# A graph network with counted edges: GpSimd waits for each count unit, the unit leaves PSUM two slots behind its last chunk, and SyncE issues the edge loads

## The chip, the core and the metric

The kernel runs on one core of a Trainium2 chip. The metric is device time in microseconds (us); the median of several executions counts. Engine names: TensorE (PE in the profile, PEld its weight load), VectorE (DVE), ScalarE (ACT), GpSimd (POOL), SyncE (SP). A name with a q behind it is the engine's sequencer, which issues DMAs.

## What is computed

Four layers of a graph network over 6,250 nodes, 100,000 edges and 128 features. Layers 0 and 1 add a message with the edge's attributes for every edge; layers 2 and 3 add the plain row of the source node.

```python
h = relu(layernorm(x))
for l in range(2):                      # layers 0, 1
    msg = relu(h[src] + edge_attr)
    agg = segment_sum(msg, dst)
    h = batchnorm((h + agg) @ W1[l] + b1[l]) * gamma[l] + beta[l]
    h = relu(relu(relu(h) @ W2[l] + b2[l]))
x = x + h
h = relu(layernorm(x))                  # layers 2, 3, twice, with a relu between
    agg = segment_sum(h[src], dst)
    h = relu(((1 + eps) * h + agg) @ wA.T + bA) @ wB.T + bB
x = x + h
```

`src` and `dst` are the same in all layers, and `dst` is sorted. This is what the count matrices use.

## The kernel before

**Turns and slots.** The edges of layers 0 and 1 are worked off in 49 turns a layer, numbered 0 to 48 in layer 0 and 49 to 97 in layer 1. A turn has four slots, a slot is 512 edges, four for each of the 128 partitions. A slot is also numbered through: slot u of turn n is 4n + u.

**Gathers.** For each slot GpSimd issues four indirect DMAs (L675), each of which fetches 128 rows of the node table into `xg`, a ring of three turns. Its only wait in a layer is that the turn three before has been summed (L672). At the start of layer 1 it waits for the table of the layer before. Two slots of each layer (slot 2 of turns 26 and 48) are left out: their rows are loaded one by one by SyncE (L573), 24 rows a turn. So a layer has 776 gathers.

**Sums and messages.** ScalarE copies a slot's edge attributes to PSUM (L759), VectorE adds the gathered rows (L1131, which waits for the slot's gathers and raises `summed`), and ScalarE applies the relu to two slots at once (L786). After the fourth slot VectorE adds the windows of an earlier turn (L1030), then builds this turn's one-hot matrix of targets (L1077). With it TensorE scatters the messages: 32 matmuls a turn (L1510, `edge_windows`). When they are done, the buffer of the attributes is free, and ScalarE issues the load for three turns later (L751, L752, `load_behind`), 1.05 MB.

**Counts for layers 2 and 3.** During layers 0 and 1 matrices are built that say how often each source occurs near each target. A chunk is 128 edges; there are 544, 274 of them in layer 0. VectorE makes the one-hot of the source rows for a turn's chunks (L1096, `src_hot`, a ring of two turns) and, in slots 1 to 3, two or three chunks' cells (L1117, a ring of six chunks in `cell_room`). TensorE multiplies the two into the four banks of `psA` (L1494, `build_counts`): four matmuls for a piece, which is a chunk, or half of one where a unit ends in its middle. A unit is a run of chunks; there are 96, 26 in layer 0 of up to 16 chunks, 70 in layer 1, of three to six. When a unit is complete, ScalarE copies it from `psA` to `count_out` (L742), and SyncE stores it (L587). The next unit's first matmul waits for that copy. `cells_used` counts the pieces that TensorE has multiplied.

**The order.** Each engine has a queue written out by hand. TensorE does, in turn n, all chunks of the turn, then the turn's scatter. ScalarE copies a unit in the slot in which its last chunk's cells are made. VectorE does, in a turn: source rows, then for each slot cells and sum, then the windows. The preparation of all indices stands ahead of layer 0's turns on VectorE and TensorE, and GpSimd gathers meanwhile.

**Between and behind.** After a layer's edges two products with the weights and a batch norm follow for all nodes, and the rows are written to the table. Layers 2 and 3 multiply the count matrices with the features (L1537) and gather only the edges that the counts leave over (L695).

## Time and profile before

| | us |
|---|---|
| median of 3 runs | 2755.7 |
| lowest and highest | 2754.37, 2758.44 |
| the profiled execution, its own time | 2753.93 |
| its span in the profile | 2752.1 |
| layer 0, GpSimd's first to last gather | 13 to 988 |
| layer 1, the same | 1032 to 2001 |
| layers 2 and 3 and what stands around them | 2001 to 2752 |

The page gives each engine's busy time, the chain of work that ended last, and groups of like instructions; the trace answers with the instructions in order of time. An engine's idle time just before an instruction is shown with what ended it; "issue" means that nothing in the profile did. Idle time of an engine that isn't the last costs nothing. The granted clock of TensorE is a share of 2.4 GHz.

### The profile page before, as it was taken

To read this page: it belongs to the slowest core of one execution; us is meant where nothing else is said; L and a number is where in the kernel's file an instruction comes from. 1 tells how busy PE (TensorE), PEld (TensorE's weight loads), DVE (VectorE), ACT (ScalarE), POOL (GpSimd) and SP (SyncE) were. 2 spreads that over 40 slices of the span, in tenths; PEclk is the share of its full clock that TensorE was granted. 3 is DMA by queue.
4 is the path that set the end of the run, shared out by engine and by line. 5 is a ranking of instruction groups with operands and counts; after the bars stand their busy time and mean duration, and the time that the engine had idled before them with its cause. 6 is when DMAs were issued, how large, how long until landed. Compare 5 with 4: busy or idle time off the path is not lost.

```text
span 2752.1 us, 35065 instructions
## 1 busy us (share of the span) xinstructions
PE 1908.3 (69%) x9399; PEld 1278.4 (46%) x9399; DVE 1701.1 (62%) x2880; ACT 735.4 (27%) x1002; POOL 1941.4 (71%) x2048
## 2 busy tenths in 40 slices
PE   2476656566656672666566666656578999989999
PEld 2354444344444442435444444434444566546555
DVE  7797677777777764777777777777774221342212
ACT  4132222222222251333333333333361000210001
POOL 6777777777777727777777777777707777377773
PEclk8687777787888786878878888888878999999999
DMA  6343433343434333444444444444426566465653
GB/s 199 97 144 107 129 107 122 113 128 114 135 114 136 120 112 98 132 138 127 149 128 149 135 156 141 156 149 149 146 92 203 190 219 198 135 208 186 211 193 101
DMA packets 228544, 396.82 MB, mean 144 GB/s; under 512 B 43080, under 2 KB 133020, under 8 KB 228388
## 3 DMA queue, kind: packets, MB, share of 16 engines
q0 software_dynamic: 65024, 133.30, 18.1%
q1 hardware_dynamic: 111684, 162.15, 17.2%
q10 hardware_dynamic: 51680, 99.63, 10.4%
q8 instruction: 57, 0.93, 0.1%
q14 instruction: 99, 0.81, 0.1%
HBM read 333.10 MB, written 61.81 MB: 143 GB/s over the span
## 4 chain that ended last, share of the span: by engine, by line
POOL 52%; PE 22%; issue 18%; DVE 4%; DMA 3%; ACT 1%; DVEq 1%; POOLq 0%; SPq 0%; ACTq 0%
POOL xg L675 50%; PE psA L1537 14%; PE psG L1552 4%; POOL xg L695 2%; DMA xg<-node_table,src_all 2%; PE psG L1601 2%; PE psA L1609 1%; DVE xp_room L1131 0%; DVE hid L1077 0%; PE psG L1631 0%; DVE acc L1030 0%; DVE hid L1247 0%; PE psA L1618 0%; DVE xp_room L955 0%; DVEq L1052 0%
## 5 line engine op out<-in xcount | busy, mean ns | idle before, releaser
L675 POOL DMA_INDIRECT xg<-node_table,src_all x1520 | 1437.3, 946 | 506.9 <-issue 458.3
L1510 PE MATMUL psG<-hid,xp_room 128*128 128x160 f32 x3072 | 614.2, 376 | 421.6 <-DVE hid L1077 411.7
L1510 PEld LDWEIGHTS psG<-hid,xp_room 128*128 128x128 f32 x3072 | 595.3, 255 | 466.3 <-issue 455.8
L1494 PE MATMUL psA<-cell_room,xp_room 128*128 128x512 f16 (+1 forms) x2336 | 551.6, 388 | 299.2 <-ACT count_out L742 253.3
L1117 DVE TENSOR_SCALAR cell_room<-psG,cell_all 128x932 f16<-128x932 int16 x1088 | 684.6, 688 | 0.0
L695 POOL DMA_INDIRECT xg<-node_table,idx x480 | 468.1, 975 | 250.6 <-issue 248.7
L759 ACT COPY psG<-xp_room 128x512 f32<-128x512 f32 x384 | 226.5, 590 | 1257.7 <-DVE xp_room L1131 1226.5
L1494 PEld LDWEIGHTS psA<-cell_room,xp_room 128*128 128x128 f16 x2336 | 230.7, 103 | 582.7 <-ACT count_out L742 287.8
L1131 DVE TENSOR_TENSOR xp_room<-psG,xg 128x512 f32<-128x512 f32 x380 | 257.3, 677 | 385.8 <-DMA xg<-node_table,src_all 372.2
L1030 DVE TENSOR_TENSOR acc<-acc,row_slot 128x38 f32 x192 | 38.7, 202 | 385.3 <-ACT row_slot L838 360.7
L1077 DVE SCALAR_TENSOR_TENSOR hid<-loc_all,round_off,psG 128x2560 f32<-128x2560 f32 x96 | 274.7, 2862 | 0.1
L1537 PE MATMUL psA<-cell_room,xp_room 128*128 128x456 f16 x1200 | 241.7, 361 | 21.8 <-DVE xp_room L1253 21.8
L1537 PE MATMUL psA<-hid,xp_room 128*128 128x456 f16 x1152 | 234.8, 364 | 0.0
L786 ACT ACTIVATE xp_room<-xp_room 128x1024 f32<-128x1024 f32 x196 | 206.0, 1052 | 7.6 <-DVE xp_room L1023 4.5
L1030 DVE TENSOR_TENSOR acc<-acc,psG 128x160 f32 x272 | 87.3, 321 | 193.2 <-issue 148.3
L1537 PEld LDWEIGHTS psA<-cell_room,xp_room 128*128 128x128 bf16 x1200 | 115.7, 97 | 142.8 <-issue 26.6
L742 ACT CAST count_out<-psA 128x1862 f16<-128x1862 f32 x96 | 163.3, 1701 | 57.1 <-PE psA L1494 57.0
L1537 PEld LDWEIGHTS psA<-hid,xp_room 128*128 128x128 bf16 x1152 | 111.8, 97 | 118.4
L1552 PE MATMUL psG<-rows_h,xg 128*128 128x160 f32 x960 | 136.3, 299 | 6.2 <-DMA xg<-node_table,idx 6.2
L1552 PEld LDWEIGHTS psG<-rows_h,xg 128*128 128x128 f32 x960 | 133.6, 190 | 10.3 <-DMA xg<-node_table,idx 7.2
L838 ACT COPY row_slot<-psA 128x456 f32<-128x456 f32 x16 | 8.6, 538 | 360.2 <-PE psA L1537 360.2
L1096 DVE TENSOR_TENSOR xp_room<-psG,src_lo_all 128x768 f16<-128x768 int16 (+2 forms) x132 | 93.2, 727 | 0.0
(156 smaller groups left out, 804.5 us busy)
## 6 DMA issues: line engine op xcount, KB each, us to landing
xp_room<-in_edge_attr_dram ACTq DMA_DIRECT2D x95, 768.0 KB
cell_room<-count_store SPq DMA_DIRECT2D x16, 2850.0 KB
count_store<-count_out SPq DMA_DIRECT2D x96, 465.5 KB
hid<-count_store SPq DMA_DIRECT2D x16, 2736.0 KB
xg<-node_table,src_all POOLq DMA_INDIRECT x1520
xp_room<-in_edge_attr_dram ACTq DMA_DIRECT2D x95, 256.0 KB
row_slot<-node_table SPq DMA_DIRECT2D x1024, 0.5 KB
hid<-node_table SPq DMA_DIRECT2D x1024, 0.5 KB
```

The source lines that it names most:

```text
L675: nc.gpsimd.indirect_dma_start(xg[:, n % XG, u, j, :], None, x if n < RAW_TURNS else table, bass.IndirectOffsetOnAxis(ap=src_all[:, s, j:j ...
L695: nc.gpsimd.indirect_dma_start(xg[:, q, u, j, :], None, table, bass.IndirectOffsetOnAxis(ap=idx[:, q, u, j:j + 1], axis=0),).then_inc(row_ ...
L742: act.copy(count_out[:, k % 2, :], psA[:, :, :].rearrange("p k c -> p (k c)")[:, 0:CB]).then_inc(count_evicted, 1)
L759: act.copy(ea_stage, ea[:, n % RING, u, :, :].rearrange("p j d -> p (j d)")).then_inc(ea_staged, 1)
L786: act.activation(half, half, ACT.Relu).then_inc(msg_ready, 1)
L1077: nc.vector.scalar_tensor_tensor(out=rows.rearrange("p u j w -> p (u j) w"), in0=loc.unsqueeze(2).broadcast_to((P, SLOTS * EPP, WIN)), sca ...
L1117: nc.vector.tensor_scalar(cells[:, c % CELL_RING, c0:c1], iota_bank[:, 0:c1 - c0], float(c0), cell_all[:, c:c + 1], ALU.add, ALU.is_equal) ...
L1131: nc.vector.tensor_tensor(ea[:, n % RING, u, :, :].rearrange("p j d -> p (j d)"), ea_stage, rows, ALU.add).then_inc(summed, 1)
L1494: last = nc.tensor.matmul(psA[:, bank, 0:w], src_hot[:, hots(n) % 2, at, :], cells[:, c % CELL_RING, c0:c0 + w], start=first, stop=end)
L1510: last = nc.tensor.matmul(psG[:, q, h * WIN:(h + 1) * WIN], ea[:, t, u, j, :], rows[:, u, j, :], start=(u == slots[0] and j == 0), stop=(u ...
L1537: last = nc.tensor.matmul(out_cols, xp[:, b, part, :], counts[h][:, :, i * CW:(i + 1) * CW], start=(b == 0 and part == 0), stop=(b == BLOC ...
L1552: last = nc.tensor.matmul(psG[:, q, h * WIN:(h + 1) * WIN], xg[:, q, u, j, :], late_hot[:, q, u * EPP + j, :], start=(u == slots[0] and j ...
```

## The change

It concerns layers 0 and 1.

- **GpSimd waits.** Each unit has a gate: the slot two behind the one in which its last chunk's cells are made, and at least two behind the gate before (`UNIT_GATE`). Before the gathers of the slot behind a gate GpSimd waits until TensorE has multiplied the unit. Where two gates stand more than six slots apart, further gates are put between them, for the chunks whose step lies two slots back (`BURST_GATE`). There are 109 gates, 39 in layer 0 and 70 in layer 1.
- **Units** are copied out by ScalarE at their gate, no longer in the slot of their last chunk.
- **TensorE** takes chunks slot by slot (`STEPS`). A piece of the next unit is moved behind the gate of the unit before. A turn's scatter stands behind the first slot of the turn that follows. Turns 0 and 1 keep their order.
- **Rings:** twelve chunks of cells (six of them in `rows_h`, for which VectorE waits until the table is written), source rows of three turns.
- **Chunks** are spread over one turn fewer; the last two turns of a layer have none.
- **SyncE** issues the attributes' loads (`load_ahead`), at a turn's start, ahead of its rows and stores.

```diff
-CELL_RING = 6
+CELL_RING = 12
+ROOM_CELLS = 6
+HOT_RING = 3
+LAG_SLOTS = 2
+LONGEST_BURST = 6
...
-COUNT_TURNS = TURNS - 1 - RAW_TURNS
+COUNT_TURNS = TURNS - 2 - RAW_TURNS
...
+def unit_gates():
+
+    gates, last = [], -1
+    for k in range(UNITS):
+        built = SLOT_OF[(UNIT_END[k] - 1) // 2]
+        stop = (built // SLOTS // TURNS + 1) * TURNS * SLOTS - SLOTS - 1
+        last = min(max(built + LAG_SLOTS, last + 2), stop)
+        gates.append(last)
+    return gates
...
+def piece_step(c, p0):
+
+    k = UNIT_OF[2 * c + p0 // HALF]
+    return max(SLOT_OF[c], UNIT_GATE[k - 1] + 1) if k > 0 else SLOT_OF[c]
...
+def burst_gates():
+
+    gates = {g: UNIT_USED[k] for k, g in enumerate(UNIT_GATE)}
+    for layer in range(2):
+        bounds = [(layer * TURNS + RAW_TURNS) * SLOTS - 1] + [g for g in UNIT_GATE if g // SLOTS // TURNS == layer]
+        for a, b in zip(bounds, bounds[1:]):
+            parts = -(-(b - a) // LONGEST_BURST)
+            for i in range(1, parts):
+                g = a + (b - a) * i // parts
+                gates[g] = max(USED_AFTER[c] for c in range(CHUNKS) if piece_step(c, PIECES[c][-1][0]) <= g - LAG_SLOTS)
+    return gates
...
 # SyncE
+            def load_ahead(n):
+
+                if not RING <= n < EDGE_TURNS:
+                    return
+                used = n - RING
+                sp.wait_ge(scattered[used % 2], sp.snap(rounds * (used // 2 + 1) + 1))
+                load_turn(n)
...
                 for n in range(layer * TURNS, (layer + 1) * TURNS):
-                    for k in units_in(turn_chunks(n)):
-                        sp.wait_ge(count_evicted, k + 1)
-                        sp.dma_start(count_store[k], count_out[:, k % 2, :]).then_inc(count_stored[k % 2], 16)
+                    load_ahead(n + 1)
                     gather_rows(layer, n % TURNS)
+                    for u in range(SLOTS):
+                        for k in units_at(n * SLOTS + u):
+                            sp.wait_ge(count_evicted, k + 1)
+                            sp.dma_start(count_store[k], count_out[:, k % 2, :]).then_inc(count_stored[k % 2], 16)
...
 # GpSimd
                     for u in range(SLOTS):
+                        if n * SLOTS + u - 1 in BURST_GATE:
+                            pool.wait_ge(cells_used, BURST_GATE[n * SLOTS + u - 1])
...
 # ScalarE
-                            if u == (SLOTS - 1 if n == RAW_TURNS else 1):
-                                load_behind(n - 1)
-                            units_out(slot_chunks(n, u))
+                            units_out(i)
...
 # VectorE
-                slot = hots(n) % 2
-                if n >= 2 and turn_chunks(n - 2):
-                    dve.wait_ge(cells_used, USED_AFTER[turn_chunks(n - 2)[-1]])
...
+                slot = hots(n) % HOT_RING
+                if n % TURNS == RAW_TURNS:
+                    dve.wait_ge(table_written, 16 * LG * (n // TURNS + 1))
+                if hots(n) > HOT_RING:
+                    dve.wait_ge(cells_used, USED_AFTER[turn_chunks(COUNTING[hots(n) - 1 - HOT_RING])[-1]])
...
 # TensorE
-                    build_counts(n)
-                    edge_windows(layer, n)
+                    for u in range(SLOTS):
+                        build_counts(n * SLOTS + u)
+                        if u == 0 and n > max(layer * TURNS, RAW_TURNS):
+                            edge_windows(layer, n - 1)
+                    if n < RAW_TURNS:
+                        edge_windows(layer, n)
+                edge_windows(layer, (layer + 1) * TURNS - 1)
```

## Rows read from the trace of the kernel before

**Rows 1.** The page: busy time by engine, then groups (busy, mean ns, idle before).

```profile
PE 1908.3 (69%) x9399; PEld 1278.4 (46%) x9399; DVE 1701.1 (62%) x2880; ACT 735.4 (27%) x1002; POOL 1941.4 (71%) x2048
...
L1494 PE MATMUL psA<-cell_room,xp_room 128*128 128x512 f16 (+1 forms) x2336 | 551.6, 388 | 299.2 <-ACT count_out L742 253.3
L1117 DVE TENSOR_SCALAR cell_room<-psG,cell_all 128x932 f16<-128x932 int16 x1088 | 684.6, 688 | 0.0
```

**Rows 2.** The page: the chain that ended last, by engine and by line.

```profile
POOL 52%; PE 22%; issue 18%; DVE 4%; DMA 3%; ACT 1%; DVEq 1%; POOLq 0%; SPq 0%; ACTq 0%
POOL xg L675 50%; PE psA L1537 14%; PE psG L1552 4%; POOL xg L695 2%; DMA xg<-node_table,src_all 2%; PE psG L1601 2%; PE psA L1609 1%; DVE xp_room L1131 0%; DVE hid L1077 0%; PE psG L1631 0%; DVE acc L1030 0%; DVE hid L1247 0%; PE psA L1618 0%; DVE xp_room L955 0%; DVEq L1052 0%
```

**Rows 3.** Groups of layer 1, 1032 to 2002 us: the gathers.

```profile
L675 POOL DMA_INDIRECT xg<-node_table,src_all x776 | 732.2, 944 | 280.0 <-issue 233.8 <-DMA node_table<-rows_h 43.8 <-DVE xp_room L1131 2.4
```

**Rows 4.** Timeline of GpSimd, layer 1's first gathers: start, us, what [idle before].

```profile
1031.87 0.94 POOL L675 DMA_INDIRECT xg<-node_table,src_all  x1 [43.76 <-DMA node_table<-rows_h]
1033.12 0.94 POOL L675 DMA_INDIRECT xg<-node_table,src_all  x1 [0.30 <-issue]
```

**Rows 5.** Timeline of GpSimd, the 48th and 49th gather of layer 0.

```profile
78.13 0.94 POOL L675 DMA_INDIRECT xg<-node_table,src_all  x1 [0.30 <-issue]
79.38 0.95 POOL L675 DMA_INDIRECT xg<-node_table,src_all  x1 [0.30 <-issue]
```

**Rows 6.** Timeline, 99 to 123 us: the sums of slots 8 and 12, the first chunks.

```profile
99.92 0.69 DVE L1131 TENSOR_TENSOR xp_room<-psG,xg 128x512 f32<-128x512 f32 x1 [8.00 <-ACT psG L759]
...
117.78 4.12 PE L1494 MATMUL psA<-cell_room,xp_room 128*128 128x512 f16 x20
...
122.28 0.67 DVE L1131 TENSOR_TENSOR xp_room<-psG,xg 128x512 f32<-128x512 f32 x1
```

**Rows 7.** Timeline, 1784 to 1808 us: the last slot of turn 86 and turn 87.

```profile
1784.68 0.94 POOL L675 DMA_INDIRECT xg<-node_table,src_all  x1 [0.30 <-issue]
...
1788.99 0.69 DVE L1131 TENSOR_TENSOR xp_room<-psG,xg 128x512 f32<-128x512 f32 x1 [3.57 <-DMA xg<-node_table,src_all]
...
1791.20 1.69 ACT L742 CAST count_out<-psA 128x1862 f16<-128x1862 f32 x1
...
1792.94 1.74 PE L1494 MATMUL psA<-cell_room,xp_room 128*128 128x512 f16 x4 [5.87 <-ACT count_out L742]
...
1795.03 6.19 PE L1510 MATMUL psG<-hid,xp_room 128*128 128x160 f32 x32 [0.35 <-DVE hid L1077]
...
1804.61 2.56 PE L1494 MATMUL psA<-cell_room,xp_room 128*128 128x512 f16 x12 [1.80 <-ACT count_out L742]
```

**Rows 8.** Windows over two of those units: busy by engine, PEclk, DMA share, GB/s.

```profile
1792.94:1794.68 1.74, 1.74 (x4) 0.44 (x4) 1.74 (x2) 0.00 (x0) 1.13 (x3) 0.50 0.48 155
1804.61:1807.17 2.56, 2.55 (x12) 1.08 (x12) 0.74 (x2) 0.43 (x1) 1.91 (x3) 1.00 1.05 394
```

**Rows 9.** Timeline, other turns: their last gather, their scatter; a unit of four pieces.

```profile
1390.16 0.94 POOL L675 DMA_INDIRECT xg<-node_table,src_all  x1 [0.30 <-issue]
...
1398.84 4.63 PE L1510 MATMUL psG<-hid,xp_room 128*128 128x160 f32 x32 [0.24 <-issue]
...
1704.97 3.35 PE L1494 MATMUL psA<-cell_room,xp_room 128*128 128x512 f16 x16 [1.80 <-ACT count_out L742]
...
1904.52 0.94 POOL L675 DMA_INDIRECT xg<-node_table,src_all  x1 [0.30 <-issue]
...
1915.31 7.47 PE L1510 MATMUL psG<-hid,xp_room 128*128 128x160 f32 x32 [6.02 <-DVE hid L1077]
```

**Rows 10.** Timeline: a turn's row loads on SyncE; the page: all DMA traffic.

```profile
1795.51 9.03 SPq L573 DMA_DIRECT2D hid<-node_table  x24
...
DMA packets 228544, 396.82 MB, mean 144 GB/s; under 512 B 43080, under 2 KB 133020, under 8 KB 228388
```

**Rows 11.** Timeline of GpSimd in layer 2: a gather behind waits.

```profile
2110.95 0.94 POOL L695 DMA_INDIRECT xg<-node_table,idx  x1 [0.87 <-issue]
```

More of the change, by code:

```diff
@@ L123, in slot_chunks @@
     return [c for i, c in enumerate(chunks) if 1 + i * (SLOTS - 1) // len(chunks) == u]
-def units_in(chunks):
-    return [UNIT_OF[e] for c in chunks for e in (2 * c, 2 * c + 1) if e + 1 in UNIT_END]
 def row_work(t):
@@ L173, in parted, with units_at @@
     return [c for c in chunks if len(PIECES[c]) > 1]
+COUNTING = [n for n in range(EDGE_TURNS) if turn_chunks(n)]
+TURN_OF = {c: n for n in COUNTING for c in turn_chunks(n)}
+SLOT_OF = {c: n * SLOTS + u for n in COUNTING for u in range(SLOTS) for c in slot_chunks(n, u)}
 def hots(n):
-    return sum(len(turn_chunks(t)) > 0 for t in range(n + 1))
+    return COUNTING.index(n) + 1
+def unit_gates():
[6 more added lines that the diff above has]
+    return gates
+UNIT_GATE = unit_gates()
+def piece_step(c, p0):
+    k = UNIT_OF[2 * c + p0 // HALF]
+    return max(SLOT_OF[c], UNIT_GATE[k - 1] + 1) if k > 0 else SLOT_OF[c]
+STEPS = {}
+for c in range(CHUNKS):
+    for p0, p1 in PIECES[c]:
+        STEPS.setdefault(piece_step(c, p0), []).append((c, p0, p1))
+def burst_gates():
[8 more added lines that the diff above has]
+    return gates
+BURST_GATE = burst_gates()
+def units_at(i):
+    return [k for k, g in enumerate(UNIT_GATE) if g == i]
 MOST_CHUNKS = max(len(turn_chunks(n)) for n in range(EDGE_TURNS))
@@ L188 @@
 LAYERS = 4
-assert TURNS % 2 == 1 and 2 * SLOTS * EPP * WIN <= CELL_RING * CB
+assert TURNS % 2 == 1 and 2 * SLOTS * EPP * WIN <= ROOM_CELLS * CB
 assert SUPERS % SLOTS == 0 and OVERLAP % EPP == 0 and SECOND <= P
@@ L193 @@
 assert CB % 2 == 0 and CB - IOTA <= IOTA <= 1024 and MOST_CHUNKS <= CELL_RING and EPP * D == 512
-assert CBANKS == 4 and UPG * CW <= 512 and HALF_B * UPG >= CELL_RING * BLOCKS // 2
+assert CBANKS == 4 and UPG * CW <= 512 and HALF_B * UPG >= ROOM_CELLS * BLOCKS // 2
 def group_blocks(g):
@@ L734, in centre_raw, with units_out @@
                     last.then_inc(raw_centred, 1)
-            def units_out(chunks):
-                for k in units_in(chunks):
+            def units_out(i):
+                for k in units_at(i):
                     act.wait_ge(cells_used, UNIT_USED[k])
@@ L1116, in chunk_cells @@
                 for c0, c1 in CELL_PARTS:
[L1117 removed]
+                    nc.vector.tensor_scalar(cells[c % CELL_RING][:, c0:c1], iota_bank[:, 0:c1 - c0],
                                             float(c0), cell_all[:, c:c + 1], ALU.add, ALU.is_equal
@@ L1475, in turn_rows, with build_counts @@
                     last.then_inc(cols_turned, 1)
-            def build_counts(n):
-                chunks = turn_chunks(n)
-                for i, c in enumerate(chunks):
-                    if i == 0:
-                        pe.wait_ge(src_hot_ready, hots(n))
-                    for p0, p1 in PIECES[c]:
-                        k = UNIT_OF[2 * c + p0 // HALF]
-                        first = 2 * c + p0 // HALF == UNIT_END[k] - UNIT_SIZES[k]
-                        end = 2 * c + p1 // HALF == UNIT_END[k]
-                        if first and k > 0:
-                            pe.wait_ge(count_evicted, k)
-                        pe.wait_ge(cells_ready, 2 * (c + 1))
-                        at = len(chunks) + parted(chunks).index(c) if p0 else i
-                        for bank in range(CBANKS):
-                            c0 = bank * 512
-                            w = min(512, CB - c0)
-                            last = nc.tensor.matmul(psA[:, bank, 0:w], src_hot[:, hots(n) % 2, at, :],
-                                                    cells[:, c % CELL_RING, c0:c0 + w], start=first, stop=end)
-                        last.then_inc(cells_used, 1)
+            def build_counts(i):
+                for c, p0, p1 in STEPS.get(i, ()):
+                    n = TURN_OF[c]
+                    chunks = turn_chunks(n)
+                    if c == chunks[0] and p0 == 0:
+                        pe.wait_ge(src_hot_ready, hots(n))
+                    k = UNIT_OF[2 * c + p0 // HALF]
+                    first = 2 * c + p0 // HALF == UNIT_END[k] - UNIT_SIZES[k]
+                    end = 2 * c + p1 // HALF == UNIT_END[k]
+                    if first and k > 0:
+                        pe.wait_ge(count_evicted, k)
+                    pe.wait_ge(cells_ready, 2 * (c + 1))
+                    at = len(chunks) + parted(chunks).index(c) if p0 else c - chunks[0]
+                    for bank in range(CBANKS):
+                        c0 = bank * 512
+                        w = min(512, CB - c0)
+                        last = nc.tensor.matmul(psA[:, bank, 0:w], src_hot[:, hots(n) % HOT_RING, at, :],
+                                                cells[c % CELL_RING][:, c0:c0 + w], start=first, stop=end)
+                    last.then_inc(cells_used, 1)
             def edge_windows(layer, n):
```

24 lines of the change are left out of this document (9 added, 15 removed).

## The prediction

> **What bounds the kernel now.** I read the page's chain first, because one engine is named in half of it: GpSimd, at the gather line of layers 0 and 1, L675, with 50% of the span; TensorE follows with 22%, nearly all of it in layers 2 and 3 [rows 2]. The busy shares do not say this: in the whole span GpSimd has 71%, TensorE 69%, VectorE 62% [rows 1]. Then I looked at the groups of layer 1 alone: 776 gathers, 732.2 us busy and 233.8 us of "issue" before them, so (732.2 + 233.8 + 2.4) / 776 = 1.248 us for each, and nothing else stands before a gather but one pause of 43.8 us [rows 3]. GpSimd thus never waits inside layer 0 or 1. A layer's time is 776 x 1.248 = 968 us plus the stretch between the last gather of one layer and the first of the next (43.76 us after layer 0 [rows 4]). Everything else in these layers is hidden: VectorE builds cells with no idle before them at all [rows 1], and TensorE's 253.3 us of waiting for ScalarE's evictions [rows 1] is idle time of an engine that is not last.
>
> So a wait put into GpSimd's queue is free only if it is already met when GpSimd comes to it. If it is not, all later gathers of the layer move, and so does the layer's end. That is the question for each of the 109 gates.
>
> **First gate.** The diff's formulas, filled in with the constants, give layer 0 39 gates (26 of units, 13 between) and layer 1 70, all of units. The first stands after slot 3 of turn 2 (slot 11): before slot 12's gathers GpSimd waits for two chunks used. Now GpSimd starts slot 12's first gather at 79.38 us: it is the 49th, after 48 of twelve slots [rows 5]. VectorE and TensorE are far behind at that point, because the preparation of indices comes first in their queues: VectorE sums slot 8 at 99.92 us and slot 12 at 122.28 us, and TensorE multiplies its first chunks from 117.78 us on, twenty matmuls in 4.12 us, so that the second chunk (eight matmuls) is used at 117.78 + 8/20 x 4.12 = 119.4 us [rows 6]. Nothing in the change brings it forward: turn 1's scatter still stands before it on TensorE, since turns 0 and 1 keep their order. GpSimd then waits 119.4 - 79.4 = **40 us**. Before the change it used this time to run up to three turns ahead, as deep as the buffers of xg allow, and VectorE caught up behind it. That lead is what the gate takes away; the gathers are the bound from then on, so nothing gives it back. Queued behind the wait are all later gathers, and VectorE waits for them.
>
> **Later gates, layer by layer.** A unit's matmuls can't begin before the unit before it is evicted, and that now happens at that unit's gate slot. Between two gates TensorE must therefore do: landing of the gate slot's gathers, VectorE's sum, ScalarE's eviction, all matmuls of the next unit, and, where a turn ends between, the scatter of 32 matmuls. GpSimd takes 8 gathers, 9.98 us, for a distance of two slots. Forty gates have this distance. I priced them with turn 86 and what follows it, taking 1785.62 us (1784.68 + 0.94, the last gather of turn 86) as zero [rows 7].
>
> Twelve gates stand after slot 2 and their predecessor after slot 0. Their unit stands behind the scatter on TensorE, which ends at 1795.03 + 6.19 = 1801.22, that is at 15.6. A late unit has three or four pieces of four matmuls; three take 2.56 us [rows 7], four take 3.35 [rows 9], mean 2.95. It is used at 18.55; GpSimd is there after three slots, 12 x 1.248 = 14.98. Loss 3.55 each, 12 x 3.55 = **43 us**. VectorE's next turn then hangs on gathers that are as much later, so the loss returns each turn.
>
> Fourteen gates (one of them layer 0's last) stand after slot 1, with the predecessor after slot 3 of the turn before. Here the unit goes ahead of the scatter, but must wait for the eviction, which ends at 1791.20 + 1.69 = 1792.89, at 7.27. After this wait TensorE is slow: a piece that follows 5.87 us of idle takes 1.74 us [rows 7], at a granted clock of 0.50 (1.2 GHz), where the next unit's three pieces, close behind a scatter, had 1.00 (2.4 GHz) and took 0.85 each [rows 8]. With pieces some 1.6 us apart, 3.5 of them end at 7.27 + 5.6 = 12.87; GpSimd is there at 9.98. Loss 2.9 each, 14 x 2.9 = **41 us**.
>
> The other fourteen of distance two come after slot 0 or 3; their eviction isn't behind a scatter, and the stall before has already given them 3 us, so I cost them at nothing, as I do all gates of three slots or more: these have 5 us more than the cases above, whose losses are under 4. If that cover were gone, each us would cost 1 us at up to 14 gates.
>
> **Bounds of these two terms.** They depend on when the gathers land and on TensorE's clock. In a turn where landing was quick and TensorE warm the scatter ended at 1398.84 + 4.63 - 1391.10 = 12.4, and a gate after slot 2 would just be met; a warm unit after slot 3 ends at 7.27 + 2.95 = 10.2, 0.2 late. So the lower end is 0. In a slow turn the scatter ended at 1915.31 + 7.47 - 1905.46 = 17.3 [rows 9]: with 3.35 behind it 5.7 late, 12 x 5.7 = 68; four slow pieces of 1.74 end at 14.2, 4.25 late, 14 x 4.25 = 60. Upper end 128. I take 84, as turn 86 is near the middle of its neighbours.
>
> The Trainium skill (TensorE: Matmul & The Clock Gate, Part 1) says that "the default state is throttled, and activity releases the throttle". It speaks against this change, which breaks TensorE's work into units with a wait before each; the piece of 1.74 us at the clock 0.50 [rows 8] agrees with it.
>
> **What costs nothing.** *Loads by SyncE:* two issues a turn leave ScalarE's queue, which isn't last. On SyncE they stand behind the count stores of the turn before and ahead of 24 row loads (9.03 us of issue [rows 10]); with them a turn fills about half of 16 x 1.248 = 20 us. The latest load is issued after an eviction behind slot 3, at about 7.3; 1.05 MB at the mean 144 GB/s [rows 10] is 7.3 us, so it lands at 15.5, and its first reader on ScalarE comes one turn after zero, at 24. If this cover were gone, ScalarE's copies would hold up the sums. *Scatters a slot later:* they wait for the marks of VectorE now, and still do. *Rings of 12 cells and 3 row marks:* VectorE has no wait to lose there [rows 1]. *One turn fewer with chunks:* VectorE builds the same number. *Ends of layers and layers 2, 3:* the last gate is six slots or more before the end, so the 43.76 us stay as they are.
>
> **Sum.** 2753.9 (profiled execution, span 2752.1) + 40 + 43 + 41 = 2878; the median of the runs is 1.8 above the profiled one: **2879 us**.
>
> **Rivals.** (a) *Only the first gate costs*: landing quick and TensorE warm in nearly all turns, the lower ends. 2755.7 + 40 = 2796. For it: turns like the one at 1391. Against: a stalled GpSimd leaves TensorE more idle. 12%. (b) *TensorE slow throughout*: scatters of 7.47 and pieces of 1.6 in layer 1. Gates after slot 2 then lose 3.55 + 1.28 + 2.65 = 7.5, 12 x 7.5 = 90; 2755.7 + 40 + 90 + 41 = 2927. This is what the clock page of the Trainium skill leads to if the waits between units always lower the clock. 7%. (c) *A met wait costs GpSimd time too*: one gather of layer 2, whose turn starts with waits, came after 0.87 instead of 0.30 [rows 11]; 109 x 0.57 = 62, 2941. Against: the waits for `summed` that stand in layers 0 and 1 already, two a turn, cost nothing in [rows 3]. 4%. (d) *Not slower: a pause quickens the gathers behind it.* If descriptors pile up in a queue and the 0.30 before each gather is that queue, a pause drains it, and the four gathers behind each gate come without it: 109 x 4 x 0.30 = 131 us back, 2879 - 131 = 2748. It decides from 0.28 us per gather on (124 / 436). Against: after a pause of 43.76 us the next gather comes 1.25 us later, as always [rows 4]. 4%. (e) *The gates are met*, so nothing changes: 2756. It needs the second chunk 40 us earlier. 3%. The forecast has 70%.
>
> **Range and chances.** From (a) to the forecast with its upper bounds: 2755.7 + 40 + 128 = 2924; so 2796 to 2924. About 0.2% is what a measurement of this kernel can tell from no change. Slower 0.93, within 0.2% 0.03, faster 0.04.
>
> **What would show it.** In the changed kernel's trace: one wait of about 40 us on GpSimd, near 79 us, released by TensorE's count matmuls; in layer 0 hardly another; in layer 1 some 25 waits of 2 to 6 us on the same line, by the end of it mostly once a turn; VectorE's idle before its sums up by the same sum; layers 2 and 3 and the ends of layers as long as now; gathers still 1.25 us apart. I am wrong if GpSimd's waits sum to under 30 us, if gathers change their pace, or if the time is lost at waits of ScalarE for loads.

## The result and the profile after

| | before | after |
|---|---|---|
| median, us | 2755.0 | 2895.0 |
| lowest and highest | 2752.2, 2758.4 | 2889.5, 2898.1 |
| span of the profiled execution | 2752.1 | 2891.7 |
| layer 0, GpSimd's first to last gather | 13 to 988 | 13 to 1021 |
| layer 1, the same | 1032 to 2000 | 1066 to 2141 |

The changed kernel takes 1.0509 times as long [1.0497, 1.0521]: 140 us more. Layer 0 is 33 us longer, layer 1 106 us; the stretch between the layers and everything behind layer 1 are as long as before, within 1.2 us. (Layer 1's last gather of before ends at 2000.4, not 2001.)

The page of after, its chain by engine and by line, then the groups of the gathers and of VectorE's sums (busy, mean ns, idle before and what ended it):

```profile
POOL 37%; PE 32%; issue 15%; DMA 8%; DVE 6%; DVEq 2%; ACT 1%; POOLq 0%; SPq 0%; ACTq 0%
POOL xg L743 35%; PE psA L1598 15%; DMA xg<-node_table,src_all 7%; PE psG L1566 6%; PE psG L1613 4%; PE psA L1550 4%; DVE hid L1133 2%; PE psG L1662 1%; POOL xg L763 1%; DVEq L1108 1%; PE psA L1670 1%; DVE acc L1086 1%; DVE xp_room L1187 0%; PE psG L1692 0%; ACT count_out L810 0%
...
L743 POOL DMA_INDIRECT xg<-node_table,src_all x1520 | 1439.1, 947 | 647.9 <-issue 449.9
...
L1187 DVE TENSOR_TENSOR xp_room<-psG,xg 128x512 f32<-128x512 f32 x380 | 257.3, 677 | 524.1 <-DMA xg<-node_table,src_all 518.8
```

The same sums in the page of before:

```profile
L1131 DVE TENSOR_TENSOR xp_room<-psG,xg 128x512 f32<-128x512 f32 x380 | 257.3, 677 | 385.8 <-DMA xg<-node_table,src_all 372.2
```

VectorE stands idle 138 us longer before its sums, which is GpSimd's lost time passed on. The gathers are L743 now. One takes 947 ns (946 before), but GpSimd holds only 37% of the chain, where it had 52% [rows 2]; TensorE has 32%, DMA 8% (3% before), VectorE 6%. So in a part of layer 1 the end is set by a chain that runs through several engines. Where GpSimd stood, its waits tell (total us, times, longest); first the stretch of layer 0 behind the preparation, then layer 1:

```profile
POOL xg L743 <- issue: 222.5, 730, 0.3
POOL xg L743 <- PE psA L1550: 35.9, 5, 32.2
```

```profile
POOL xg L743 <- issue: 226.2, 742, 0.3
POOL xg L743 <- PE psA L1550: 114.7, 30, 7.0
```

"issue" is the 0.30 us ahead of each gather that [rows 3] showed. Behind TensorE's count matmuls (L1550) GpSimd now waits 35.9 us in layer 0, 32.2 of them at one gate, and 114.7 us at 30 gates of layer 1. Less the usual 0.30 each, that is 34.4 + 105.7 = 140 us, the whole difference. In what follows "layer 1's waits" is this sum, less 0.30 for each.

**The first gate.** The timeline at the gate that stands behind slot 11 (start, us, what, [idle before]):

```profile
84.52 0.59 ACT L818 COPY psG<-xp_room 128x512 f32<-128x512 f32 x1 [8.95 <-DVE first_i L1100]
...
90.56 0.67 DVE L1187 TENSOR_TENSOR xp_room<-psG,xg 128x512 f32<-128x512 f32 x1
...
108.00 4.92 PE L1550 MATMUL psA<-cell_room,xp_room 128*128 128x512 f16 x24
...
110.02 0.94 POOL L743 DMA_INDIRECT xg<-node_table,src_all  x1 [32.23 <-PE psA L1550]
111.27 0.94 POOL L743 DMA_INDIRECT xg<-node_table,src_all  x1 [0.30 <-issue]
```

VectorE sums slot 8 at 90.56 us, where it stood at 99.92 before, and the second chunk is used at about 110, where 119.4 was worked out from [rows 6]. The wait is 32.2 us.

**One turn of layer 1.** From one gate behind slot 2 to the next, a turn later:

```profile
1867.74 1.71 ACT L810 CAST count_out<-psA 128x1862 f16<-128x1862 f32 x1 [1.53 <-PE psA L1550]
1867.97 0.94 POOL L743 DMA_INDIRECT xg<-node_table,src_all  x1 [6.75 <-PE psA L1550]
...
1869.47 0.37 SPq L654 DMA_DIRECT2D count_store<-count_out  x1
...
1869.89 0.43 SPq L615 DMA_DIRECT2D xp_room<-in_edge_attr_dram  x1
1870.36 0.71 SPq L616 DMA_DIRECT2D xp_room<-in_edge_attr_dram  x1
...
1871.71 0.94 POOL L743 DMA_INDIRECT xg<-node_table,src_all  x1 [0.30 <-issue]
...
1877.94 0.69 DVE L1187 TENSOR_TENSOR xp_room<-psG,xg 128x512 f32<-128x512 f32 x1 [9.92 <-DMA xg<-node_table,src_all]
...
1879.99 0.78 DVE L1086 TENSOR_TENSOR acc<-acc,psG 128x160 f32 x2 [1.35 <-issue]
...
1880.82 2.86 DVE L1133 SCALAR_TENSOR_TENSOR hid<-loc_all,round_off,psG 128x2560 f32<-128x2560 f32 x1
...
1883.98 6.11 PE L1566 MATMUL psG<-hid,xp_room 128*128 128x160 f32 x32 [11.91 <-DVE hid L1133]
...
1889.93 2.55 PE L1550 MATMUL psA<-rows_h,xp_room 128*128 128x512 f16 x12
...
1893.13 0.95 POOL L743 DMA_INDIRECT xg<-node_table,src_all  x1 [5.49 <-PE psA L1550]
```

This is the chain, and it closes on itself. The gate opens at 1867.97. Slot 3's four gathers end at 1871.71 + 0.94 = 1872.65. They land at 1877.94, 5.3 us later, when VectorE can add them. Windows and one-hot matrix take until 1883.98, the scatter and the three pieces of the next unit until 1889.93 + 2.55 = 1892.48, and GpSimd goes on at 1893.13: 25.16 us for a turn whose 16 gathers need 16 x 1.248 = 19.97. Waits of 6.75 and 5.49 us at gates one turn apart show that the loss doesn't die away; each late slot 3 makes the next unit late. Note the two loads of SyncE (L615, L616), issued while slot 3 is being gathered: they stand behind the store of the unit (L654), which waits for ScalarE's copy of it (L810), which TensorE's last piece releases together with the gate. Windows of the gathers' own time and of the landing (us, busy by engine with counts, PEclk, DMA share, GB/s):

```profile
1867.97:1872.65 4.68, 2.53 (x12) 1.10 (x12) 0.05 (x1) 1.48 (x1) 3.77 (x4) 1.00 0.53 140
1872.65:1877.94 5.29, 0.00 (x0) 0.00 (x0) 0.00 (x0) 0.00 (x0) 3.77 (x5) 0.90 0.80 253
```

In the 5.29 us of landing no engine but GpSimd works; the DMA engines are 0.80 busy with 253 GB/s.

### The profile page after: what moved, and what is told of

Same layout as the page of the kernel before. It is cut to its first block, busy times and chain, and to the rows that moved or that the text cites. A ratio compares the mean times of both kernels' runs of the same rounds, so it can differ in the third digit from the quotient of the medians.

```text
span 2891.7 us, 35118 instructions
## 1 busy us (share of the span) xinstructions
PE 1882.2 (65%) x9399; PEld 1265.4 (44%) x9399; DVE 1700.1 (59%) x2878; ACT 733.3 (25%) x1002; POOL 1939.4 (67%) x2048
## 4 chain that ended last, share of the span: by engine, by line
POOL 37%; PE 32%; issue 15%; DMA 8%; DVE 6%; DVEq 2%; ACT 1%; POOLq 0%; SPq 0%; ACTq 0%
POOL xg L743 35%; PE psA L1598 15%; DMA xg<-node_table,src_all 7%; PE psG L1566 6%; PE psG L1613 4%; PE psA L1550 4%; DVE hid L1133 2%; PE psG L1662 1%; POOL xg L763 1%; DVEq L1108 1%; PE psA L1670 1%; DVE acc L1086 1%; DVE xp_room L1187 0%; PE psG L1692 0%; ACT count_out L810 0%
## 5 line engine op out<-in xcount | busy, mean ns | idle before, releaser
L743 POOL DMA_INDIRECT xg<-node_table,src_all x1520 | 1439.1, 947 | 647.9 <-issue 449.9
L1566 PE MATMUL psG<-hid,xp_room 128*128 128x160 f32 x3072 | 588.2, 365 | 639.4 <-DVE hid L1133 610.3
L1566 PEld LDWEIGHTS psG<-hid,xp_room 128*128 128x128 f32 x3072 | 570.5, 245 | 669.6 <-issue 636.8
L1550 PE MATMUL psA<-rows_h,xp_room 128*128 128x512 f16 (+1 forms) x1156 | 284.3, 401 | 144.5 <-ACT count_out L810 126.0
L1550 PE MATMUL psA<-cell_room,xp_room 128*128 128x512 f16 (+1 forms) x1180 | 276.3, 385 | 112.8 <-ACT count_out L810 96.9
L1173 DVE TENSOR_SCALAR cell_room<-psG,cell_all 128x932 f16<-128x932 int16 (+1 forms) x548 | 345.1, 686 | 0.0
L1173 DVE TENSOR_SCALAR rows_h<-psG,cell_all 128x932 f16<-128x932 int16 (+1 forms) x540 | 340.3, 686 | 0.0
L1550 PEld LDWEIGHTS psA<-rows_h,xp_room 128*128 128x128 f16 x1156 | 120.4, 107 | 293.0 <-ACT count_out L810 134.4
L1550 PEld LDWEIGHTS psA<-cell_room,xp_room 128*128 128x128 f16 x1180 | 118.7, 103 | 250.4 <-ACT count_out L810 104.5
L810 ACT CAST count_out<-psA 128x1862 f16<-128x1862 f32 x96 | 163.0, 1698 | 13.5 <-PE psA L1550 13.5
```

What stands on the lines that cost most here:

```text
L743: nc.gpsimd.indirect_dma_start(xg[:, n % XG, u, j, :], None, x if n < RAW_TURNS else table, bass.IndirectOffsetOnAxis(ap=src_all[:, s, j:j ...
L810: act.copy(count_out[:, k % 2, :], psA[:, :, :].rearrange("p k c -> p (k c)")[:, 0:CB]).then_inc(count_evicted, 1)
L1173: nc.vector.tensor_scalar(cells[c % CELL_RING][:, c0:c1], iota_bank[:, 0:c1 - c0], float(c0), cell_all[:, c:c + 1], ALU.add, ALU.is_equal) ...
L1550: last = nc.tensor.matmul(psA[:, bank, 0:w], src_hot[:, hots(n) % HOT_RING, at, :], cells[c % CELL_RING][:, c0:c0 + w], start=first, stop=end)
L1566: last = nc.tensor.matmul(psG[:, q, h * WIN:(h + 1) * WIN], ea[:, t, u, j, :], rows[:, u, j, :], start=(u == slots[0] and j == 0), stop=(u ...
```

## The experiments

The ratio is to the kernel before, timed beside each. Layer 1's waits as above, from the one profiled execution of each kernel; the first gate took 29 to 34 us in all kernels that keep the change's gates and SyncE's loads.

| kernel | median, us | ratio, interval | layer 1's waits |
|---|---|---|---|
| after | 2895.0 | 1.0509 [1.0497, 1.0521] | 105.7 |
| e1_no_gates | 2755.2 | 1.0005 [0.9995, 1.0014] | none |
| e2_first_gate | 2795.6 | 1.0147 [1.0130, 1.0163] | none |
| e4_gates_late | 2776.9 | 1.0082 [1.0065, 1.0099] | none |
| e3_loads_scalar | 2868.4 | 1.0417 [1.0396, 1.0437] | 65.7 |
| e5_sync_early | 2875.4 | 1.0429 [1.0411, 1.0446] | 81.1 |
| e8_small_loads | 2843.4 | 1.0326 [1.0309, 1.0343] | 54.4 |
| e11_short_scatters | 2879.2 | 1.0453 [1.0436, 1.0471] | 76.5 |
| e12_both_small | 2839.3 | 1.0304 [1.0287, 1.0322] | 47.3 |
| e9_warm_scatters | 2953.2 | 1.0725 [1.0707, 1.0743] | 154.2 |
| e10_warm_units | 2910.9 | 1.0565 [1.0547, 1.0583] | 117.5 |
| e6_three_rows | 2748.3 | 0.9968 [0.9957, 0.9980] | none |
| e7_four_rows | 2848.0 | 1.0325 [1.0308, 1.0343] | other waits |

### Do GpSimd's waits cost it all?

**The change without them:**

```diff
 # after
-                        if n * SLOTS + u - 1 in BURST_GATE:
-                            pool.wait_ge(cells_used, BURST_GATE[n * SLOTS + u - 1])
```

> The changed kernel without GpSimd's 109 waits; all the rest of the change stays (evictions at the gate slots, scatters a slot later, loads by SyncE, the larger rings). Theory A (the whole loss is GpSimd standing at its gates): 2755 us, within 4 us of the kernel before, and no wait before a gather but the one between the layers. Theory B (the new order of TensorE and the late evictions cost time by themselves): over 2775 us, with VectorE or TensorE in the chain of the edge layers in place of the gathers.

It took 2755.15 us, 1.4 more than before, and the interval of the ratio includes 1. So later evictions, scatters a slot later, the longer rings and SyncE's loads cost nothing that can be told from noise (0.14% at most, 4 us) as long as GpSimd does not wait. That holds only for a GpSimd that runs ahead; the loads come back below.

**The first wait alone,** in the kernel before:

```diff
 # before
+                        if n * SLOTS + u == 12:
+                            pool.wait_ge(cells_used, 2)
```

> The kernel before with one wait added: before the gathers of slot 12 GpSimd waits for two pieces used. Theory A (lead that is lost at the start is never given back, the gathers being the bound): the wait ends when the second chunk is used, 119.4 us in the kernel before, so 40 us of wait and 2755 + 40 = 2795 us. Rival (the layer has slack behind its start, VectorE being far behind anyway): much of it is given back, 2760 to 2775 us.

GpSimd's wait in its trace:

```profile
POOL xg L677 <- PE psA L1496: 41.6, 1, 41.6
```

41.6 us of waiting, and 2795.57 - 2753.77 = 41.8 us of time: a wait at 79 us is paid in full, and nothing in the 2,700 us behind it gives it back. This kernel keeps ScalarE's loads, and its wait is the 40 us of the prediction; the change's is 32.2.

**All waits two slots later:**

```diff
 # after
-                        if n * SLOTS + u - 1 in BURST_GATE:
-                            pool.wait_ge(cells_used, BURST_GATE[n * SLOTS + u - 1])
+                        if n * SLOTS + u - 3 in BURST_GATE:
+                            pool.wait_ge(cells_used, BURST_GATE[n * SLOTS + u - 3])
```

> The changed kernel with each of GpSimd's waits two slots later (four slots behind the last chunk); evictions and TensorE's order as in the changed kernel. Theory A: a wait that is met costs nothing, and two slots (9.98 us) are more than any loss of a later gate (6.5 us), so only the first gate costs, and there GpSimd comes 10 us later to a count that is reached at 109.7 us: 21 us of wait, 2755 + 21 = 2776 us. Theory B (waits or order cost by themselves): over 2800 us.

2776.9. The first gate waits 22.5 us; before no other is GpSimd idle for more than its usual 0.30. So a wait that is met costs GpSimd nothing, at over a hundred gates, and the loss of layer 1 is a matter of less than two slots (10 us) at each gate.

### Why layer 1 lost more than it should: the loads

The gathers of slot 3 landed later than in [rows 7]. Theory C puts this on SyncE's loads, theory D on TensorE's clock. Landing is counted from the end of a slot's last gather to the sum's start, mean of slot 3 in turns 85 to 96: 3.39 us before, 4.93 after.

**Loads by ScalarE again,** at their old place:

```diff
 # after, SyncE
-                    load_ahead(n + 1)
...
 # ScalarE
+                            if u == (SLOTS - 1 if n == RAW_TURNS else 1):
+                                load_behind(n - 1)
                             units_out(i)
```

> The changed kernel with the attributes' loads back on ScalarE, at their old place behind the scatter; the gates stay. Theory C (the twelve gates after slot 2 lose 5.5 us each in place of 3.55 because SyncE's load now starts with the released gathers and slot 3's gathers land late): landing of slot 3 in the last turns back from 4.9 to 3.4 us behind the last gather, some 1.5 to 2 us less at each of 12 gates and about 10 us less at the others, but the first gate back to 40 us from 32, since VectorE's first sums stand behind ScalarE's wait for the first scatter again: 2895 - 18 - 10 + 8 = 2875 us. Theory D (TensorE's clock is what makes the gates late): only the first gate changes, 2903 us.

2868.4: 26.6 us less than the change. Landing falls to 2.27 us, layer 1's waits from 105.7 to 65.7, while the first gate rises to 41.9, as in the kernel with the first wait alone (41.6). So the new issuer of the loads costs layer 1 40 us and gives 9 back at the start.

**Loads by SyncE, but earlier,** ahead of the count stores of the turn:

```diff
 # after, SyncE
-                    load_ahead(n + 1)
                     gather_rows(layer, n % TURNS)
                     for u in range(SLOTS):
+                        if u == 1:
+                            load_ahead(n + 2)
```

> The changed kernel with SyncE's load moved ahead of the turn's count stores: it is issued in turn n for turn n + 2, as soon as turn n - 1 is scattered, on the same queue of SyncE. Theory C1 (the time of issue is what counts: behind the last eviction the load runs beside the gathers that have just been released): landing of slot 3 and the waits of layer 1 as with the loads on ScalarE (66 us in place of 106), the first gate as in the changed kernel (32 us): 2895 - 40 = 2855 us. Theory C2 (the queue is what counts: loads, rows and stores behind one another on SyncE): no change, 2895 us.

2875.4, between the two. Landing is shorter than in the change and with ScalarE's loads, 1.90 us, so it is the load's moment that held up slot 3, not the engine that issues it. But only 25 of the 40 us come back: gates behind slot 1 lose 39.6 us here and lost 9.9 in the change. Slot 3's gain was partly another slot's loss.

The moment can be read in six of the traces. Here is turn 87 of the kernel before, slot 3's first gather and ScalarE's load:

```profile
1800.90 0.94 POOL L675 DMA_INDIRECT xg<-node_table,src_all  x1 [0.30 <-issue]
1801.26 0.39 ACTq L751 DMA_DIRECT2D xp_room<-in_edge_attr_dram  x1
```

Means of turns 85 to 94, us; the load's issue is counted from the start of slot 3's first gather (its last one ends 4.7 behind that start):

| kernel | load issued | landing of slot 3 |
|---|---|---|
| e3_loads_scalar | 2.4 ahead | 2.38 |
| e5_sync_early | 2.4 ahead | 1.94 |
| before | 1.2 behind | 3.63 |
| after | 2.1 behind | 5.15 |
| e4_gates_late | 5.0 behind | 1.91 |
| e1_no_gates | 5.3 behind | 2.37 |

Where the load goes out ahead of the four gathers or behind their end, they land in about 2 us; where it goes out among them, in 3.6 and 5.2. The kernel before had such loads too; the change put them 0.9 us later. These kernels differ in their waits as well, so the table alone does not show the cause. That called for taking the load's traffic away altogether.

**Loads an eighth as large,** at the change's own place:

```diff
 # after, SyncE
+                parts = 16 if n >= TURNS + RING else P
-                sp.dma_start(ea[:, t, 0:SLOTS - 1, :, :].rearrange("p u j d -> p u (j d)"), slots).then_inc(ea_loaded[t], 16)
+                sp.dma_start(ea[0:parts, t, 0:SLOTS - 1, :, :].rearrange("p u j d -> p u (j d)"), slots[0:parts]).then_inc(ea_loaded[t], 16)
```

and the same for the fourth slot.

> The changed kernel, except that in layer 1, from its fourth turn on, a load of attributes fetches 16 of the 128 partitions, so an eighth of its bytes and packets (the other partitions keep what the turn three before left there: seven eighths of the attributes are left out). Issue, waits and order stay. Theory C (what layer 1 loses is mostly the landing of slot 3's gathers, which the load's packets hold up): landing falls to 1.9 us or below, as with the early load, and now for the whole turn; at least the 40 us between the change (2895) and the kernel with ScalarE's loads come back, and as the other slots' landing is freed too, some 15 more: 2840, with layer 1's waits at 50 us. Rival (the load's bytes don't matter, only its place in a queue): 2895.

2843.4, 51.6 us less than the change, and layer 1's waits are 51.3 us shorter. The same stretches as above, in this kernel (slot 3's gathers after a gate, then their landing):

```profile
1842.46:1847.15 4.69, 2.53 (x12) 1.10 (x12) 1.95 (x4) 1.78 (x2) 3.77 (x4) 1.00 0.48 156
1847.15:1849.71 2.56, 0.00 (x0) 0.00 (x0) 0.00 (x0) 0.00 (x0) 1.88 (x2) 1.00 0.40 80
```

Landing takes 2.56 us where it took 5.29, at a DMA share of 0.40 instead of 0.80; both are turn 86. GpSimd's waits in layer 1:

```profile
POOL xg L744 <- PE psA L1551: 61.9, 25, 4.1
```

The issue, the waits and the order are the change's own; only the packets of the loads are gone. So these packets hold up the gathers that GpSimd has just been let go to issue: half of layer 1's loss. The Trainium skill (DMA: Bandwidth & Descriptors, Queues, rings and completion order) says that each DMA engine takes turns between the queues it has work for, a packet at a time. That would make a gather's packets share with a load's, and the landing of 5.29 and 2.56 us agrees. No run here shows whether the two share the engines or another part of the way.

### What of it is TensorE's clock?

**TensorE kept busy ahead of the scatter.** The bank may be written once VectorE has added its windows, so that wait comes first:

```diff
 # after, TensorE
+                    pe.wait_ge(window_added, pe.snap((rounds * n + r) * WINDOWS + (layer * 2 * WINDOWS + WINDOWS + 1)))
+                    for _ in range(32 if layer == 1 and n > TURNS + 2 else 0):
+                        nc.tensor.matmul(psG[:, q, 384:512], ident[:, :], ident[:, :], start=True, stop=True,
+                                         skip_group_check=True)
                     pe.wait_ge(hot_set[q], pe.snap(rounds * (n // 2) + r + (spare_sets(layer, q) + 1)))
-                    pe.wait_ge(window_added, pe.snap((rounds * n + r) * WINDOWS + (layer * 2 * WINDOWS + WINDOWS + 1)))
```

> The changed kernel; in layer 1, from its fourth turn on, TensorE multiplies the identity with itself 32 times (into columns of the window's bank that nothing uses) before each scatter, while it waits for VectorE's one-hot matrix. Extra work of 3.6 us at the full clock, beside an idle time of 316 us in 31 turns. Theory D (the low clock of the scatter carries part of the twelve gates behind slot 2): scatters go from 5.94 us (30 of 48 above 6) to 4.6, the twelve gates lose 1.4 us less each: 2895 - 17 = 2878. Rival: the extra work ends after the one-hot matrix in the turns with little idle time, and what is late there is given back: 2895 to 2915.

2953.2, far slower than either theory said. One turn of it:

```profile
1922.03 2.86 DVE L1133 SCALAR_TENSOR_TENSOR hid<-loc_all,round_off,psG 128x2560 f32<-128x2560 f32 x1
...
1922.04 10.13 PE L1561 MATMUL psG<-ident 128*128 128x128 f32 x64 [9.28 <-DVE acc L1086]
...
1932.00 4.51 PE L1569 MATMUL psG<-hid,xp_room 128*128 128x160 f32 x32
```

The scatter is at its full speed, 4.51 us at a granted clock of 1.00 (2.4 GHz), but 32 products of f32 are 64 matmuls in the trace and take 10.13 us, and they can't begin before the windows are added at 1922.03. The one-hot matrix is there at 1924.89; the scatter begins 7.1 us behind it. The loss was put on the chain, not taken off it.

**TensorE kept busy ahead of units** that start in slot 0:

```diff
 # after, TensorE
                     if first and k > 0:
+                        if i >= (TURNS + 3) * SLOTS and i % SLOTS == 0:
+                            done = i // SLOTS - 1
+                            pe.wait_ge(window_added, pe.snap(rounds * done * WINDOWS + (2 * WINDOWS + WINDOWS + 1)))
+                            for _ in range(16):
+                                nc.tensor.matmul(psG[:, done % 2, 384:512], ident[:, :], ident[:, :], start=True, stop=True,
+                                                 skip_group_check=True)
                         pe.wait_ge(count_evicted, k)
```

> The changed kernel; in layer 1, from its fourth turn on, TensorE multiplies the identity with itself 16 times (into columns of the window's bank that nothing uses) before the first piece of each unit that starts in slot 0, while it waits for ScalarE's copy of the unit before; ahead of that it waits until VectorE has added the windows of three turns before. 1.8 us at the full clock, 3.6 at half, beside an idle time of 5 to 7 us. Theory D (the low clock of pieces and scatter carries the loss behind such a copy): the pieces behind it take 0.85 us instead of 1.4 to 1.7 and the scatter behind them 4.5 instead of 6 to 7.5, so gates after slots 1 and 2 lose 2 to 3 us less: 2895 - 26 x 2 = 2843. Rival C (landing and the order of the work set it, the clock little): 2885 to 2895; if the multiplications themselves keep the clock low or end after the copy, 2895 to 2910.

2910.9. The extra products are busy for 90.3 us in layer 1, with twice as many matmuls as were meant, and gates behind slot 1 lose 45.4 us instead of 9.9. Neither run says what the clock costs, because each made TensorE late by more than a warm clock could give.

**Shorter scatters** instead, with no work added: 24 of 32 matmuls.

```diff
 # after, TensorE
+                parts = EPP - 1 if n >= TURNS + RING else EPP
...
-                            for j in range(EPP):
+                            for j in range(parts):
...
```

> The changed kernel, except that in layer 1, from its fourth turn on, a scatter takes three of a partition's four edges in each slot: 24 matmuls instead of 32 (a quarter of the messages is left out of the sums). In turns 85 to 96 a scatter of the change took 6.64 us, at the full clock it takes 4.5; 24 matmuls at the low clock would take 4.98. So this run gives TensorE nearly what a warm clock would, without extra work. Theory D (the low clock of the scatter carries part of the loss behind slot 2): twelve gates lose 1.7 us less each, 2895 - 20 = 2875. Rival (the gates wait for landing and sums, the scatter hides): 2893 to 2897.

2879.2: 15.8 us less, most of the 20 expected. The runs lie from 2871.3 to 2884.1, and the profiled one is the fastest. In it the twelve gates behind slot 2 lose 51.8 us instead of 66.1, 1.2 less each, and layer 1's waits are 29.2 us shorter in all: behind slot 3 they fall from 25.8 to 6.3, behind slot 1 they rise from 9.9 to 18.5. So the scatter's length lies on the chain, and with it what the low clock adds to it.

**Both cuts:**

> Both cuts: in layer 1, from its fourth turn on, loads of 16 of 128 partitions and scatters of 24 of 32 matmuls (seven eighths of the attributes and a quarter of the messages are left out). If landing and scatter are two terms of one path, their savings add: 2843 with small loads alone, less the 20 us of the short scatters: 2823, with layer 1's waits at about 33 us. If they hide behind each other, 2838 to 2843.

2839.3: only 4.1 us below the small loads alone, with intervals that touch. The savings do not add. The traces say why, at the twelve gates behind slot 2. From the end of a turn's last gather to GpSimd's start behind that gate there are four legs: the landing, the time from the sum to the scatter (windows and one-hot matrix), the scatter, and the rest (the unit, and until GpSimd starts). With the gate met GpSimd would start after 12 x 1.248 + 0.30 = 15.28 us. Means of the twelve, us:

| kernel | landing | to the scatter | scatter (granted clock) | the rest | sum less 15.28 | loss at the gate |
|---|---|---|---|---|---|---|
| after | 5.28 | 6.01 | 6.66 (0.69) | 2.85 | 5.52 | 5.51 |
| e11_short_scatters | 5.44 | 6.01 | 5.29 (0.66) | 2.85 | 4.31 | 4.31 |
| e8_small_loads | 2.59 | 6.00 | 6.68 (0.68) | 2.85 | 2.84 | 2.83 |
| e12_both_small | 2.54 | 6.01 | 6.03 (0.57) | 2.85 | 2.15 | 2.14 |

So landing and scatter are two legs of one path, and nothing hides. But with both cuts the shorter scatter ran at a lower mean clock, so it saved 0.65 us where it had saved 1.37. Layer 1's waits are 7.1 us shorter than with small loads alone; against that the first gate waited 33.5 us in this kernel's profile and 31.0 there.

### A way that does gain

GpSimd's pace sets layers 0 and 1 [rows 3], so fewer gathers should be time. Before had two slots a layer loaded as rows by SyncE. **Three:**

```diff
 # before
-ROW_TURNS = (26, TURNS - 1)
+ROW_TURNS = (19, 34, TURNS - 1)
-BY_SYNC = 6
+BY_SYNC = 9
```

> The kernel before, with three slots of each layer loaded row by row by SyncE in place of two (36 rows a turn in place of 24), so that GpSimd has 4 gathers fewer in each layer. Theory A (the number of gathers is all that sets the time of layers 0 and 1): 2 x 4 x 1.248 = 10 us less, 2744 us. Rival (VectorE's or SyncE's queue is right behind the gathers): 2750 us or more.

2748.3 us, 0.9968 of before [0.9957, 0.9980], so a small gain that is clear of noise: 8 gathers less, 8.7 us of the 10 expected. **Four** (`ROW_TURNS = (15, 26, 37, TURNS - 1)`, `BY_SYNC = 12`):

> The kernel before with four such slots (48 rows a turn; at 9.03 us per 24 rows and some 2.7 us of reading addresses ahead of them SyncE needs about 23 us a turn of 20). Theory A with SyncE's time: GpSimd would save 20 us, but rows that come late hold up the sums of their slots: 2740 to 2800 us; if SyncE's issue were no limit, 2734 us.

2848.0, 91 us slower than before. GpSimd's long waits in its trace:

```profile
POOL xg L695 <- issue: 301.3, 471, 118.5
POOL xg L675 <- DMA node_table<-rows_h: 80.1, 1, 80.1
POOL xg L675 <- DVE xp_room L1131: 28.7, 18, 9.9
```

The stretch between the layers has grown from 43.8 [rows 4] to 80.1, 28.7 us are spent waiting for sums (23.3 of them beyond the usual 0.30), and one gap in layer 2 of 118.5 us was 65.9 before. Together, 36.3 + 23.3 + 52.6 less 20 us for 16 gathers, they make 92 us where 91 were lost. SyncE waits for ScalarE's copies only twice in the whole of layer 1, 87.5 us in all and 79.1 of them at once, where it waited 42 times and 253.3 us with three rows: it issues rows and stores almost without a pause and runs behind. The price of a row is SyncE's time, and at four slots it is used up. Which of SyncE's late transfers makes the gap in layer 2 was not traced.

## Why the prediction was right, and where it wasn't

Forecast were 2879 us in a range of 2796 to 2924; it took 2895. Sign and place are right: the waits on GpSimd cost everything, no gather changed its pace, and the rest of the change alone costs nothing.

- **First gate, 40 us: 32.2.** The mechanism and its full price stand: alone it cost 41.8. The step that failed is "Nothing in the change brings it forward". In [rows 6] the sum of slot 8 waited 8.00 us for ScalarE, whose copy of the attributes stood behind its load for turn 3, and that load behind turn 0's scatter. The change takes this load out of ScalarE's queue, so the copy starts at 84.52 and the sum comes 9.4 us earlier. With the loads back on ScalarE the wait is 41.9. I had put down the removal as worthless since ScalarE "isn't last"; just there it was. In the trace of before, turn 0's scatter, the load and the copy follow one another:

```profile
92.18 6.00 PE L1510 MATMUL psG<-hid,xp_room 128*128 128x160 f32 x32 [9.95 <-DVE hid L1077]
...
98.21 0.44 ACTq L751 DMA_DIRECT2D xp_room<-in_edge_attr_dram  x1
...
99.30 0.59 ACT L759 COPY psG<-xp_room 128x512 f32<-128x512 f32 x1 [22.46 <-issue]
```

- **Twelve gates behind slot 2, 43 us: 66.1.** All twelve wait, 5.5 us each instead of 3.55, and each turn again, as forecast. The term was mis-sized by landing: turn 86's 3.37 us was taken [rows 7], but ahead of these gates it is 5.28 in the mean (the first line of the table of four legs). That is 1.9 of the 1.95 us by which each gate loses more.
- **Fourteen gates behind slot 1, 41 us: 11.8** (five in layer 1 with 9.9, one in layer 0). All eight that were met in layer 1 come two slots behind a gate after slot 3 that had itself just waited, 1.4 to 4.0 us. So the step that failed is "I cost them at nothing": twelve **gates behind slot 3** lost 25.8 and one behind slot 0 lost 4.0. Ten of the thirteen are gates of three slots (23.5 us), whose cover of 5 us was gone: the last line below is released by a unit of five pieces (4.13 us) behind a scatter of 7.60 whose turn's last gathers had taken 5.8 us to land. Both groups together lost 41.6 where 41 was forecast, but mostly at other gates and for another reason, so the sum was right there by luck.

```profile
1597.65 7.60 PE L1566 MATMUL psG<-hid,xp_room 128*128 128x160 f32 x32 [8.47 <-DVE hid L1133]
...
1605.08 4.13 PE L1550 MATMUL psA<-cell_room,xp_room 128*128 128x512 f16 x20
...
1609.86 0.94 POOL L743 DMA_INDIRECT xg<-node_table,src_all  x1 [4.32 <-PE psA L1550]
```

- **Loads by SyncE, nothing: about 40 us in layer 1.** I asked whether a load would arrive in time for its reader; it does: ScalarE never waits for one in layer 1. I did not ask what it meets on its way. SyncE has the load queued behind the store of the last unit, and that unit is what GpSimd's gate waits for too. So the gate lets the gathers and the load go at nearly the same moment (1867.97 and 1869.89). In the kernel before the load followed the scatter; it met slot 3 too, but earlier in it, and GpSimd did not wait for what followed.
- **Two slips in the sums.** The load's landing at 15.5: 7.3 + 7.3 make 14.6. A warm scatter's 12.4 + 2.95 is 0.4 past 14.98, so that gate would not "just be met" and the lower end of the two terms was some 7 us instead of 0. Neither changes the forecast.
- **Rivals.** Met waits are free (gates two slots later), which ends (c). The pace is 947 ns with waits and without, which ends (d). (a) and (e) needed gates that are met. (b), TensorE slow throughout, gave 2927 and needed scatters of 7.47 us: in turns 85 to 96 a scatter took 6.64 in the mean, 6.59 in the kernel before, both at a mean granted clock of 0.69 (0.50 is 1.2 GHz, 1.00 is 2.4). So the gates did not slow the scatters there. What that clock costs is bounded only: a scatter at the full clock takes 4.5, so warm scatters could give at most 12 x 2.1 = 26 of the 66.1 us; the shorter scatters gave 14.3 of them.
- **Not settled:** how the 54.4 us that layer 1 still loses without the loads' packets divide between TensorE's clock and the order of the work. 34.0 of them are lost at the twelve gates behind slot 2, where scatters at the full clock could give back at most 12 x 2.2 = 26, by the table of four legs; 20.4 are lost behind slot 1, where no such sum was made. A warm TensorE without longer work was not tried.

## What to carry to other kernels

A wait put on the engine that sets the pace is paid in full unless it is already met; moving it by two slots was worth 118 us here (2895 to 2777), and nothing behind the first gate gave a lost microsecond back. When a wait paces an engine, ask which other queues are released by the same event: a transfer that starts among others can lengthen their landing (5.3 us instead of 2.6 here), and a latency that was hidden while the engine ran ahead is now on the chain. Before adding extra work to keep an engine warm, look for when it can start and how many instructions the trace will count.

## What I had not expected of the hardware

- The landing of a slot's last gather depends on what else moves: 2.56 us at a DMA share of 0.40, 5.29 us at 0.80, with the same gathers.
- A gather by GpSimd keeps its 0.94 us and the next one its 0.30 behind every one of the change's waits in layers 0 and 1, from 0.8 to 45 us: the pace has no memory.
- A scatter of 32 matmuls took 4.51 us behind 10.13 us of matmuls (the turn of e9_warm_scatters above) at a granted clock of 1.00 (2.4 GHz), and 6.11 behind 11.91 us of idle time in the change's, at a mean of 0.74. The Trainium skill (TensorE: Matmul & The Clock Gate, Part 1) has activity release the throttle, and these rows agree. The two windows, the change first (us, busy by engine with counts, PEclk, DMA share, GB/s):

```profile
1883.98:1890.09 6.11, 6.11 (x33) 6.01 (x34) 6.11 (x11) 3.81 (x4) 2.83 (x3) 0.74 0.36 124
1932.00:1936.51 4.51, 4.51 (x35) 4.41 (x34) 2.86 (x5) 0.59 (x1) 0.00 (x0) 1.00 0.00 0
```

- Work cut from a scatter came back in part through the clock: with small loads, 24 matmuls took 6.03 us at a granted clock of 0.57 where 32 took 6.68 at 0.68.
